# Adding v and gate times bias by accumulating DMAs: a two-sublayer adaLN kernel on one core

## The reference

```python
h = layernorm(x) * (1 + ca) + sa
x = x + ga * attention(h)          # heads of 16 of 32 lanes: only the first 16 tokens of a batch matter
h = layernorm(x) * (1 + cb) + sb
x = x + gb * ffn(h)
# ffn: x and weight are quantised in blocks of 32 to a 6-bit grid with a scale, then
# out = xd @ wd.T + bias
```

## Time and profile before

| | |
|---|---|
| median of the runs | 385.32 us |
| profiled execution | 385.07 us, span 382.8 us |
| TensorE / weight load busy | 322.2 us (84%) / 245.4 us |
| VectorE busy | 290.9 us (76%) |
| GpSimd busy | 233.8 us (61%) |
| ScalarE busy | 219.9 us (57%) |
| DMA moved | 68.10 MB, 178 GB/s over the span |
| chain that ended last | TensorE 49%, VectorE 22%, issue 8%, ScalarE 7%, GpSimd 7%, DMA 4% |

### The profile page before, as it was taken

One profiled execution on the slowest core, in us unless ns is written; L12 is line 12 of the kernel. 1 busy time (PEld: TensorE's weight loads), 2 busy tenths in 40 slices (PEclk: granted clock), 3 DMA queues, 4 the chain that ended last, 5 costly groups with the idle time before them and its releaser, 6 DMA issues.

```text
span 382.8 us, 6288 instructions
## 1 busy us (share of the span) xinstructions
PE 322.2 (84%) x2302; PEld 245.4 (64%) x2302; DVE 290.9 (76%) x500; ACT 219.9 (57%) x498; POOL 233.8 (61%) x139
## 2 busy tenths in 40 slices
PE   2950065886899999999999998989999999995994
PEld 0100012664799887778888776878887878674883
DVE  2893397598764698498969877999886799799533
ACT  2001858483755787688695968767874877120310
POOL 2004886929969569675995887596956693800100
...
GB/s 262 388 406 332 96 74 197 142 196 308 200 176 87 300 106 225 100 288 158 172 176 211 217 118 239 176 197 141 242 161 167 222 165 68 45 0 110 33 133 82
DMA packets 23156, 68.10 MB, mean 178 GB/s; under 512 B 2563, under 2 KB 2692, under 8 KB 19022
## 3 DMA queue, kind: packets, MB, share of 16 engines
...
q0 software_dynamic: 7392, 14.68, 24.8%
...
## 4 chain that ended last, share of the span: by engine, by line
PE 49%; DVE 22%; issue 8%; ACT 7%; POOL 7%; DMA 4%; SPq 1%; DVEq 0%; POOLq 0%; ACTq 0%
PE ps L591 9%; PE ps L592 9%; PE ps L596 9%; PE ps L574 5%; PE ps L548 3%; DVE XL L982 3%; PE ps L672 3%; PE ps L587 3%; DMA v_bc<-mod_scratch 2%; POOL U L329 2%; POOL U L331 2%; DVE amax L1001 2%; DVE WL L989 2%; DVE X L1034 1%; PE ps L603 1%
## 5 line engine op out<-in xcount | busy, mean ns | idle before, releaser
L591 PE MATMUL ps<-WH,XH 128*128 128x512 f32 x256 | 103.0, 402 | 0.7 <-ACT XH L392 0.7
L592 PE MATMUL ps<-WL,XH 128*128 128x512 f32 x256 | 102.6, 401 | 0.0
L329 POOL TENSOR_TENSOR U<-U,c_bc 128x1024 f32<-128x1024 f32 x32 | 78.3, 2447 | 31.6 <-ACT U L408 31.6
L392 ACT ACTIVATE XH<-ps 128x512 fp32r<-128x512 f32 x64 | 37.9, 593 | 86.2 <-PE ps L574 86.1
L331 POOL TENSOR_TENSOR U<-U,sb_bc 128x1024 f32<-128x1024 f32 x32 | 76.8, 2398 | 2.5
L982 DVE TENSOR_TENSOR XL<-ps,XH 128x512 fp32r<-128x512 f32 x64 | 44.0, 688 | 45.1 <-ACT XH L392 42.5
L596 PE MATMUL ps<-WH,XL 128*128 128x512 f32 x256 | 69.7, 395 | 1.0 <-DVE XL L982 1.0
L408 ACT ACTIVATE U<-X,nmr,rstd 128x512 f32<-128x512 f32 x64 | 48.6, 810 | 21.0 <-DVE nmr L997 21.0
L592 PEld LDWEIGHTS ps<-WL,XH 128*128 128x128 f32 x256 | 49.5, 193 | 11.4
L419 ACT ACTIVATE unused<-X 128x512 bf16<-128x512 f32 x64 | 39.5, 620 | 29.6 <-POOL X L320 27.7
L596 PEld LDWEIGHTS ps<-WH,XL 128*128 128x128 f32 x256 | 48.5, 190 | 12.2 <-DVE XL L982 1.7
...
## 6 DMA issues: line engine op xcount, KB each, us to landing
...
X<-mod_scratch POOLq DMA_DIRECT2D x14, 1024.0 KB, 11.6
...
```

The costliest lines, as they stand in the source:

```text
L329: nc.gpsimd.tensor_tensor(a, a, spread(c_bc[:, b % 2, :]), ALU.mult).then_inc(u_done, 1)
L591: M(bank, XH[:, n % 2, r], WH[:, b % 2, k, :], start=False, stop=False)
L592: M(bank, XH[:, n % 2, r], WL[:, b % 2, k, :], start=False, stop=False)
```

## The change

Three things change.

1. For groups 6 to 15 x is no longer loaded by SyncE and v added to it. ScalarE fills the slot with v (`fill`, two operations of 128 x 1024 per group, in steps 4g - 18 and 4g - 17), after waiting for the slot's store; GpSimd then issues x as an accumulating DMA from DRAM, in 8 KB pieces. v of the batch has to be in SBUF for this, so SyncE loads v_bc for batches 3 to 7 (256 KB each, five loads). Groups 0 to 5 get x and v as before.
2. gb * bias is no longer a matmul. SyncE writes each batch's row four times in a row to DRAM (`gbias`), and after `modulate(g)` GpSimd issues an accumulating DMA of it onto the slot (`add_bias`), in 8 KB pieces, for all 16 groups. VectorE waits for it before it adds the group's first tile. The 64 matmuls L587 are gone, and so are G2, its two VectorE operations L831 and L833, its writes and its loads.
3. In the beginning SyncE writes GBIAS and gbias as soon as `gate` has made them. `high_part(0)` and `low_part(0)` no longer wait for the writes of G2.

```diff
+        def additions(g, bias):
+            return 2 * (g // XSLOTS) + (g % XSLOTS >= 2) + bias
...
-                if g >= XSLOTS:
-                    sp.wait_ge(stored[g % XSLOTS], 16 * (g // XSLOTS))
...
-            sp.wait_ge(g2_rows, 2)
-            sp.dma_start(mod_dram[:, GBH, :], XH[0:B, 0, :].bitcast(F32)).then_inc(g2_rows_out, 16)
-            sp.dma_start(mod_dram[:, GBL, :], XL[0:B, 0, :].bitcast(F32)).then_inc(g2_rows_out, 16)
-            sp.wait_ge(g2_rows_out, 32)
-            for b in range(2):
-                load_g2(b)
+            sp.wait_ge(gb_row, 1)
+            sp.dma_start(mod_dram[:, GBIAS, :], mrow[GBIAS]).then_inc(scratch_out, 16)
+            sp.dma_start(gbias_dram, mrow[GBIAS].unsqueeze(1).to_broadcast([B, TILES, D])).then_inc(gbias_out, 16)
...
-                if t % 2 == 0 and 2 <= t and t + 2 < GROUPS:
-                    sp.wait_ge(y_done, TILES * t)
-                    load_g2((t + 2) // 2)
-                if 1 <= t and t + 5 < GROUPS:
-                    load_x(t + 5)
+                if t % 2 == 0 and t + XSLOTS < GROUPS:
+                    b = (t + XSLOTS) // 2
+                    if b == 4:
+                        sp.wait_ge(x1_done, 4)
+                    elif b > 4:
+                        sp.wait_ge(filled, 4 * (b - 4))
+                    mod_row(v_bc[:, b % 2, :], b, V, v_in[b % 2])
...
             def add_attn_bias(g):
                 b = g // 2
-                pool.wait_ge(x_in[g % XSLOTS], 16 * (g // XSLOTS + 1))
+                if g >= XSLOTS:
+
+                    pool.wait_ge(filled, 2 * (g - XSLOTS + 1))
+                    nc.gpsimd.dma_start(X1[:, g % XSLOTS, :, :], xg[g],
+                                        accum_op=ALU.add).then_inc(x_added[g % XSLOTS], 16)
+                    return
+                pool.wait_ge(x_in[g], 16)
                 if b > 0:
-
                     pool.wait_ge(v_row_out, 16)
-                    nc.gpsimd.dma_start(X1[:, g % XSLOTS, :, :],
+                    nc.gpsimd.dma_start(X1[:, g, :, :],
                                         mod_dram[b:b + 1, V, :].unsqueeze(1).to_broadcast([P, TILES, D]),
-                                        accum_op=ALU.add).then_inc(x_summed[g % XSLOTS], 16)
+                                        accum_op=ALU.add).then_inc(x_added[g], 16)
                     return
                 pool.wait_ge(v_in[0], 16)
                 for h in range(2):
-                    a = X1[:, g % XSLOTS, HALF * h:HALF * (h + 1), :]
-                    nc.gpsimd.tensor_tensor(a, a, spread(v_bc[:]), ALU.add).then_inc(x1_done, 1)
+                    a = X1[:, g, HALF * h:HALF * (h + 1), :]
+                    nc.gpsimd.tensor_tensor(a, a, spread(v_bc[:, 0, :]), ALU.add).then_inc(x1_done, 1)
+
+
+            def add_bias(g):
+                if g == 0:
+                    pool.wait_ge(gbias_out, 16)
+                pool.wait_ge(z_done, TILES * (g + 1))
+                nc.gpsimd.dma_start(X1[:, g % XSLOTS, :, :].rearrange("p j d -> p (j d)"),
+                                    gbias_dram[g // 2].rearrange("j d -> (j d)").unsqueeze(0).to_broadcast([P, TILES * D]),
+                                    accum_op=ALU.add).then_inc(x_added[g % XSLOTS], 16)
...
                 modulate(g)
+                add_bias(g)
...
+            def fill(g, h):
+                b = g // 2
+                if h == 0:
+                    act.wait_ge(v_in[b % 2], 16 * (b // 2))
+                    act.wait_ge(stored[g % XSLOTS], 16 * (g // XSLOTS))
+                A.activation(X1[:, g % XSLOTS, HALF * h:HALF * (h + 1), :],
+                             v_bc[:, b % 2, :].unsqueeze(1).to_broadcast([P, HALF, D]), ACT.Identity).then_inc(filled, 1)
...
+                    if (g := due(q, 18 - h)) is not None and g >= XSLOTS:
+                        fill(g, h)
...
-                    pe.wait_ge(g2_in[b % 2], 16 * (b // 2 + 1))
-                if n == 0:
-                    pe.wait_ge(cleared, 4)
                 if n >= 2:
                     pe.wait_ge(o_done, n - 1)
-                M(bank, onesr[:], G2[:, b % 2, :], start=True, stop=False)
                 pe.wait_ge(xh_done, n + 1)
                 for k in range(NC):
                     r = slice(k * P, (k + 1) * P)
-                    M(bank, XH[:, n % 2, r], WH[:, b % 2, k, :], start=False, stop=False)
+                    M(bank, XH[:, n % 2, r], WH[:, b % 2, k, :], start=k == 0, stop=False)
...
-                dve.wait_ge(gb_row, 1)
-                W_.tensor_copy(XH[0:B, 0, :], mrow[GBIAS]).then_inc(g2_rows, 1)
-                dve.wait_ge(g2_rows, 1)
-                TT(XL[0:B, 0, :], mrow[GBIAS], XH[0:B, 0, :].bitcast(F32), ALU.subtract).then_inc(g2_rows, 1)
...
                 dve.wait_ge(y_done, n + 1)
+                if j == 0:
+                    dve.wait_ge(x_added[g % XSLOTS], 16 * additions(g, 1))
```

More of the change, by code:

```diff
@@ L24 @@
 XSLOTS = 6
-V, C, SB, GB, GBIAS, CA, SA, GA, GBH, GBL = range(10)
+V, C, SB, GB, GBIAS, CA, SA, GA = range(8)
 FIRST, LAST = -17, TILES * GROUPS
@@ L59, in build @@
         Wd = sb("Wd", [P, NC, D])
-        G2 = sb("G2", [P, 2, D], F32R)
         onesr = sb("onesr", [P, P], F32R)
         LR = sb("LR", [P, 2, D], F32R)
-        v_bc = sb("v_bc", [P, D])
+        v_bc = sb("v_bc", [P, 2, D])
         c_bc = sb("c_bc", [P, 2, D])
@@ L139, in build @@
         x_in = [sem(f"x_in{i}") for i in range(XSLOTS)]
-        x_summed = [sem(f"x_summed{i}") for i in range(XSLOTS)]
+        x_added = [sem(f"x_added{i}") for i in range(XSLOTS)]
         stored = [sem(f"stored{i}") for i in range(XSLOTS)]
@@ L144, in build @@
         sb_in = [sem(f"sb_in{i}") for i in range(2)]
-        g2_in = [sem(f"g2_in{i}") for i in range(2)]
         wmod_in = [sem(f"wmod_in{i}") for i in range(6)]
@@ L153, in build @@
          msp_in, msp2_in, head_stored, cleared, zeroed, dve_step, v_row_done, v_row_out, cs_rows_done,
-         cs_rows_out, g2_rows_out) = (sem(n) for n in (
+         cs_rows_out) = (sem(n) for n in (
              "c_loaded", "small_in", "vec_in", "w_in", "head_in", "xs_in", "lna_in", "bo_in", "wq_in", "wk_in", "wv_in",
              "wo_in", "scratch_out", "msp_in", "msp2_in", "head_stored", "cleared", "zeroed", "dve_step",
-             "v_row_done", "v_row_out", "cs_rows_done", "cs_rows_out", "g2_rows_out"))
-        (exp_c, silu_done, mod_mm, mod_cp, gb_row, g2_rows, rows2_done, gb_mm, gb_cp, wd_done, wscaled, wt_mm,
+             "v_row_done", "v_row_out", "cs_rows_done", "cs_rows_out"))
+        (exp_c, silu_done, mod_mm, mod_cp, gb_row, gbias_out, rows2_done, gb_mm, gb_cp, wd_done, wscaled, wt_mm,
          wt_high, wt_low, var_done, std_done, hs_done, hT_mm, hT_cp, q_mm, k_mm, v_mm, q_ready, kT_ready,
@@ L249, in _ @@
             sp.dma_start(mod_dram[:, GB, :], mrow[GB]).then_inc(scratch_out, 16)
-            sp.dma_start(mod_dram[:, GBIAS:GA + 1, :], late[0:B, :, :]).then_inc(scratch_out, 16)
-            sp.wait_ge(scratch_out, 32)
+            sp.dma_start(mod_dram[:, CA:GA + 1, :], late[0:B, CA - GBIAS:, :]).then_inc(scratch_out, 16)
+            sp.wait_ge(scratch_out, 48)
             for b in range(B):
@@ L414, in sums @@
                 else:
-                    act.wait_ge(x_summed[g % XSLOTS], 16 * (g // XSLOTS + (g % XSLOTS < 2 and -1 or 0) + 1))
+                    act.wait_ge(x_added[g % XSLOTS], 16 * additions(g, 0))
                 for j in range(HALF * h, HALF * (h + 1)):
@@ L495, in _ @@
             act.wait_ge(v_row_out, 16)
-            act.dma_start(v_bc[:], mod_dram[0:1, V, :].to_broadcast([P, D])).then_inc(v_in[0], 16)
+            act.dma_start(v_bc[:, 0, :], mod_dram[0:1, V, :].to_broadcast([P, D])).then_inc(v_in[0], 16)
             act.wait_ge(cs_rows_done, 1)
@@ L976, in low_part @@
             def low_part(n):
-                if n == 0:
-                    dve.wait_ge(g2_rows_out, 32)
                 if n >= 2:
```

12 lines of the change are left out of this document (4 added, 8 removed).

## The result

The changed kernel takes 390.98 us (median of 4 runs, 389.58 to 392.82), the kernel before 385.19 us beside it: 1.016 times as long, 95% interval 1.0107 to 1.0211. I forecast 383 us with a range of 371 to 400. The time lies in the range and the direction is wrong: slower by 1.6%, where a little faster was the likeliest. The profiled execution took 392.82 us, the longest of the four, with a span of 391.0, 8.2 us more than the span before; the medians differ by 5.8 us only, so the trace shows some 2 us more than the usual loss.

A forecast was written before the change was run, and what follows sets the result against it. TensorE was taken to bound the kernel, busy 84% of the span, with VectorE and ScalarE not far behind. From 385.1 us, -7.5 (bias matmul) + 2.5 (fills) + 3.0 (beginning) = -2.0 gave 383 us, range 371 to 400.

The forecast's parts named there:

- The beginning: Loads of x for groups 3 and 4 slowed beside bias DMAs: +3.0 us, bounds -1.7 and +8.7.
- the gain of 1.7 us: In the beginning, without L831 and L833, x of group 3 would be asked for 1.7 us earlier.
- The bias matmul: Removing 64 matmuls L587 of 0.31 us on TensorE would save 7.5 us; bounds 0 and 19.8.
- three quarters of 9.8: Share of L587's 9.8 us on the chain taken as saved, 7.5 us, VectorE or ScalarE being late next.
- The fills: Twenty ScalarE fills of 1.04 us, 20.8 us, one in eight on the chain: +2.5 us; bounds 0 and 24.8.
- three tiles later: Modulation starts some 2 us later, but its consumers, the maxima, stand about three tiles later: nothing counted; uncovered, 21 us.
- The wait for the store: It moves from SyncE to ScalarE's fill: nothing beyond the fills' 2.5 us while stores land as before.
- my rival: ScalarE waits for stores landing 10.4 us after issue, at six groups' fills, costing 12 us: 395 us; chance 0.22.
- The DMA engines: Accumulating 8 KB pieces taken at 5 us per MB: a steady group needs 15.0 of 17.3 us of DMA.
- the third rival: The DMA engines are full: 8 KB pieces cost 7.0 us per MB, giving 399 us; chance 0.14.
- GpSimd's issue: Fifteen more DMA issues, 128 pieces taking 0.33 to 1.29 us each: 5 to 21 us more on GpSimd.
- My signs of being wrong: Steady group not between 17.2 and 18.6 us, or VectorE waiting for x_added at a group's first tile.

The follow-up runs named there:

- e5: The changed kernel, but batch 0 (groups 0 and 1) takes its bias by the matmul of the kernel before; 384.8 us, ratio 0.9996.
- e9: Only the bias half of the change (x and v as before, no fills), with batches 0 and 6 by the matmul; 382.1 us, ratio 0.9894.
- e7: The changed kernel with both halves of a fill in the earlier step 4g - 18; 388.6 us, ratio 1.0099.
- e13: The changed kernel with the bias added in 512 pieces of 2 KB instead of 128 of 8 KB; 389.2 us, ratio 1.0120.
- e3: Only the bias half of the change: bias by DMA, x and v as in the kernel before, no fills; 386.9 us, ratio 1.0028.
- e15: As e3, but every group's bias added in 2 KB pieces instead of 8 KB; 390.5 us, ratio 1.0135.
- e11: As e7 (both halves of a fill in one step), with batches 0 and 6 taking the bias by the matmul; 381.4 us, ratio 0.9887.
- e12: As e9, but each bias DMA in 512 pieces of 2 KB instead of 128 of 8 KB; 378.4 us, ratio 0.9832.
- e14: As e11, but with the bias in 2 KB pieces; 381.8 us, ratio 0.9921.
- e17: The same kernel as e9 (8 KB pieces), timed again beside e18 on the same chip; 380.0 us, ratio 0.9857.
- e18: The same kernel as e12 (2 KB pieces), timed again beside e17 on the same chip; 380.1 us, ratio 0.9856.
- e4: Only the fill half of the change: fills and x by accumulating DMA from group 6, bias matmul as before; 387.9 us, ratio 1.0046.
- e2: The changed kernel with both halves of a fill one step later in ScalarE's list; 395.0 us, ratio 1.0237.
- e1: The changed kernel with the bias DMAs of groups 0 and 1 issued one group later; 389.7 us, ratio 1.0111.

## Why the prediction was wrong

I forecast -2.0 us and the trace has +8.4 at tile 63. Of the 10.4 us between them 5.4 arose in the beginning, 3.5 in tiles 7 to 50, 2.3 at tile 51, and the rest gave 0.8 back.

**The beginning** is the first step that failed, in size: +3.0 us forecast, between -1.7 and +8.7, and +8.4 measured at tile 7 (4.3 to 9.6 in the other kernels with these DMAs). I had the mechanism and both ends, and took half of a range although the kernel before already has the DMA engines 0.88 and 0.90 busy in 80 to 100 us. Even that half is 5.2 - 1.7 = 3.5 us, not 3.0. e5 removes 6.2 us of the loss, and in e9 GpSimd's waits for x end nearly as before (65.56 and 86.19 us). Not in my sum at all was TensorE's clock: with 20 matmuls in 90 to 100 us it was granted 0.66 there, and tile 4 ran at 1.2 GHz, 1.6 us. And the gain of 1.7 us was 0.5, since I misread: the product before the last takes 5.47 us there and not the 3.6 of the last. It ran behind a wait of 26 us and at a granted clock of 0.50 (before, 50 to 55 us, columns as in the earlier trace rows):

```profile
50.00:55.00 5.00, 4.02 (x9) 1.15 (x10) 4.90 (x4) 3.23 (x9) 4.92 (x3) 0.50 0.56 75
```

So TensorE came to its last product at 56.8 us by its own work, whether gb_cp was there or not.

**The bias matmul** was mis-sized. 0.31 us from the matmul to its successor is the price of the first place behind the transposes, which the next matmul then paid; the saving is 0.23 us. 4 x 0.23 = 0.9 us a group, not 1.2. From tile 7 to tile 50 43 x 0.23 = 9.9 us could be won. e7 wins 6.4 and e13 6.0, but both start 6.9 us behind, and kernels that start late win more (e3 5.3, e15 4.7). Those that start at most 2 us behind and have no long wait for a store (e9, e11, e12, e14, e17, e18) win 3.1 to 4.6. In the last twelve tiles, 51 to 63, e9 wins nothing (-2.7 and -2.6), though eight of them have no bias matmul. The chain runs over VectorE there (before, 339.8 to 351.9 us), and behind it TensorE works at 1.2 GHz, in e9 for all eight products of a tile at 0.43 us, before for five of nine. So "three quarters of 9.8" was too much: a third to a half of 9.9 came back where neither the beginning nor a store was in the way. I also called all four stretches of the earlier trace rows almost only TensorE's, which fits the first two; in the last two "issue", ScalarE and VectorE stand between.

**The fills** were sized right, 20 of 1.05 us against 1.04, and misjudged in place. I counted one in eight on the chain. The chain does run through ScalarE and VectorE in 192 to 237 us, but to tile 39 that cost nothing that shows. GpSimd stands 37.6 us before the x DMAs, which I had covered with "three tiles later"; this sum by itself is no loss, e4 has 45.1 us of it and loses 1.8. e7 moves one half and wins 6.4 instead of 1.5 us to tile 50; with batches 0 and 6 by the matmul the same move wins 4.3 instead of 2.7 in the traces, and 3.2 us in the times. So the place of `fill(g, 1)` cost 1.7 to 4.9 us. e2 moves both halves the other way, and the maxima wait 21.3 instead of 16.6 us.

**The wait for the store** I had put at nothing in the sum, and that step failed too: it is where the change and e7 part. From tile 39 to tile 50 the change loses 1.7 us, while e3, e7 and e9 win 2.7 each. There were two waits of 6.4 us in all, where my rival needed six and 12 us, and the second cost most of it. The median landing was 5.2 us, the one that hurt 11.7. My rival's time, 395 us, is what e2 took, for another reason.

**The DMA engines.** In 60 to 62 us q0 has them alone:

```profile
q0 software_dynamic: 48, 0.39, 97.0%
```

2 x 16 x 0.97 / 48 = 647 ns for an accumulating 8 KB piece, 5.2 us per MB: I had taken 5, and the third rival (7.0) is out. The Trainium skill ("Collectives: The Full Stack", in "The bandwidth ceiling: the fold count and why AG ≠ RS ≠ AR") counts an add as the traffic of two copies. An estimate by that page is 2 x 276 = 552 ns: too little by 15%. In 100 to 310 us the queues take 61.2 and 23.5%, 84.7% (73.2% before; my 15.0 of 17.3 us is 87%):

```profile
q0 software_dynamic: 3770, 23.48, 61.2%
q1 hardware_dynamic: 4410, 16.88, 23.5%
```

The average was right and hid what mattered: the beginning at 1.0 and more, and the single store that took 11.7 us.

**GpSimd's issue** of 128 pieces takes 0.88 us, between my ends of 0.33 and 1.29; with 2 KB pieces it is 1.30 (e13), as in the earlier trace rows. 26 issues of 0.88 and 4 of 1.3 in place of 14 of 1.3 are some 10 us more (16 issues more, not the fifteen that I wrote); none of it was seen on the chain by itself.

**The gap at tile 50** no step of mine had. That TensorE stops for 1 to 6 us where nothing is waited for, in most kernels with a bias DMA and in none without one, is shown by the traces; that a bias DMA issued 12 us ahead makes it longer rests on three pairs of single traces. What it waits for is not shown. A late fetch of its instructions would look like this: the gap always comes behind the same 111 of the 128 matmuls in after, e1, e2, e3, e7, e13 and e15, and behind 105 to 109 in the kernels with other code, and the profile has one packet of the instruction queue in 317 to 321 us. But the kernel before has one at this place too and no gap. The cause stays open.

**My signs of being wrong** missed it. The group took 18.5 us from tile 7 to tile 50, between 17.2 and 18.6, and VectorE never waited for x_added: by these two I was right. Both look at the steady part only, and the first product, which I had 3 us later, came 3.3 us earlier (65.76 us, before 69.02).

**The sum as it came out**: beginning +8.4, tiles 7 to 50 -1.5, tile 51 +2.3, the rest -0.8: +8.4 at tile 63 and +8.2 in the span.
